# Second graph layer: attributes turned in three pieces, one-hots in PSUM in all rows, last norm in place

## What is computed

```python
gathered = x[edge_col] * edge_vals[:, None]
pre_embed = segment_sum(gathered, edge_row, num_segments=N)
x = layernorm(x + pre_embed @ W.T)              # first layer: not touched by the change
summand = tensor_product(x[src], edge_attr_9, [w0, w1, w2, w3, w4])
x = layernorm(x + segment_sum(summand, dst, N) / sqrt(10))   # second layer
```

## Time and profile before

| what | value |
| --- | --- |
| median of 3 runs | 4139.94 us (4139.83 to 4140.0) |
| the profiled execution's own time | 4139.79 us |
| its span in the profile | 4138.0 us |
| second layer, first to last gather | 1529.47 to 4113.40 us |
| busy over the span: POOL, PE, DVE, ACT | 67%, 58%, 51%, 34% |

### The profile page before, as it was taken

The page is one execution under the profiler, slowest core; times in us unless marked ns, Lnnn a source line. Parts: engine busy times, 40 slices in busy tenths (PEclk is TensorE's granted clock), DMA queues, the critical chain, the costliest instruction groups (busy, mean ns, idle before and its releaser), DMA issues.

```text
span 4138.0 us, 55255 instructions
## 1 busy us (share of the span) xinstructions
PE 2400.2 (58%) x15332; PEld 2126.9 (51%) x15334; DVE 2119.9 (51%) x4357; ACT 1420.4 (34%) x2142; POOL 2769.7 (67%) x2887
## 2 busy tenths in 40 slices
PE   2200199999999964555455554545555455555454
PEld 1000199999999954444444444444444444444443
DVE  8999888888888872232222332322332222323433
ACT  5444366666666651121121211211121111212222
POOL 5100077777777737777777777777777777777775
PEclk6555599999999966677776776767667766776767
DMA  1000133333333332221221222222221221212222
GB/s 58 8 0 20 63 97 96 97 96 98 96 96 92 96 115 59 53 59 53 58 58 53 58 58 53 58 58 53 58 58 53 58 58 52 58 53 73 79 75 57
DMA packets 116447, 268.24 MB, mean 65 GB/s; under 512 B 50449, under 2 KB 50593, under 8 KB 115233
## 3 DMA queue, kind: packets, MB, share of 16 engines
q0 software_dynamic: 92080, 191.02, 17.4%
q1 hardware_dynamic: 19698, 68.09, 4.7%
q10 hardware_dynamic: 4608, 8.39, 0.5%
HBM read 252.30 MB, written 8.72 MB: 63 GB/s over the span
## 4 chain that ended last, share of the span: by engine, by line
POOL 42%; issue 16%; PE 4%; DMA 1%; POOLq 0%; DVE 0%; ACT 0%; DVEq 0%
POOL feat L1565 42%; PE quad L1730 3%; PE mixed L1742 1%; DMA feat<-x,ids 1%; POOLq L1561 0%; POOLq L1562 0%; PE attr_t L1690 0%; ACT z_last L1669 0%; DVE group L1878 0%; DVE dst_col L1965 0%; POOLq L1555 0%; DVE z_last L1976 0%; DVE stats L1979 0%; PE y L1754 0%; POOLq L1559 0%
## 5 line engine op out<-in xcount | busy, mean ns | idle before, releaser
L1565 POOL DMA_INDIRECT feat<-x,ids x2048 | 1960.3, 957 | 636.3 <-issue 632.3
L1730 PE MATMUL quad<-attr_hot,feat 128*128 128x144 f32 x4096 | 919.8, 407 | 1229.4 <-DMA feat<-x,ids 644.3
L1730 PEld LDWEIGHTS quad<-attr_hot,feat 128*128 128x128 f32 x4096 | 860.5, 294 | 1292.9 <-issue 1286.6
L1878 DVE TENSOR_TENSOR group<-group,quad 128x504 f32 (+1 forms) x512 | 347.9, 679 | 1725.5 <-PE quad L1730 1681.5
L1137 POOL DMA_INDIRECT l_feat<-in_x,id_of x768 | 727.7, 948 | 601.7 <-ACT w_of L830 366.4
L1582 ACT ACTIVATE quad<-quad 128x1008 uint32<-128x1008 uint32 x258 | 256.6, 995 | 1834.0 <-DVE group L1878 1834.0
L1742 PE MATMUL mixed<-group,mix 128*128 128x384 f32 x1152 | 414.9, 518 | 17.9 <-DVE group L1878 17.9
L1039 DVE TENSOR_SCALAR keys<-swap,src_of,w_of 128x184 f32<-128x184 f32 x1024 | 327.1, 389 | 93.5 <-PE l_pre L1230 93.5
L1039 DVE TENSOR_SCALAR w_row<-swap,src_of,w_of 128x184 f32<-128x184 f32 x1024 | 327.6, 390 | 51.4 <-PE l_pre L1230 49.7
L1742 PEld LDWEIGHTS mixed<-group,mix 128*128 128x128 f32 x1152 | 235.4, 209 | 171.7 <-issue 49.5
L1211 PE MATMUL got<-x_near,far_w 128*128 128x128 bf16 x4224 | 301.0, 220 | 11.0 <-ACT far_w L847 11.0
(11 more groups left out here) (252 smaller groups left out, 2428.7 us busy)
## 6 DMA issues: line engine op xcount, KB each, us to landing
place<-table SPq DMA_DIRECT2D x64, 640.0 KB
feat<-x,ids POOLq DMA_INDIRECT x2048, 2.5
l_feat<-in_x,id_of POOLq DMA_INDIRECT x768
attr_in<-in_edge_attr SPq DMA_DIRECT2D x18, 576.0 KB, 3.8
norm_x<-in_x SPq DMA_DIRECT2D x16, 256.0 KB, 2.7
x<-norm_z ACTq DMA_DIRECT2D x16, 256.0 KB, 2.4
x_t<-x SPq DMA_DIRECT2D x15, 256.0 KB, 2.7
out<-z_t ACTq DMA_DIRECT2D x15, 256.0 KB, 2.1
```

Source lines behind the costliest of these rows:

```text
L1565: pool.indirect_dma_start(feat[z][:, t, :], None, x1, bass.IndirectOffsetOnAxis(ap=ids[j // (O // 2)][:, c:c + 1], axis=0),).then_inc(feat ...
L1730: last = nc.tensor.matmul(bank[:, :, bass.ds(places[t % H], WIN)], feat[z % S][:, t, :], attr_hot[z % 2][:, t, :, :], start=False, stop=(t ...
L1878: nc.vector.tensor_tensor(to, to, quad[:, q, 0:NA * QUAD_WIN].rearrange("p (m n) -> p m n", m=NA), ALU.add).then_inc(quad_added, 1)
```

## The change

SBUF work space is given up: `off_f` now lies in `attr_hot[0]`, `tile_offs` in `tile_start` itself, `x_last` in `x_t[1]`, and `late_hot`, `z_t` and `z_last` are gone. `attr_t` shrinks from two PSUM banks to one, and the bank won becomes `hots_at`, which holds `hot` and `iota` in all rows, late ones too. The eight attribute matrices are turned four at a time: the first four in row 4 as before, the other four (`turn_rest`) between the halves of row 6, after ScalarE has emptied the bank in row 5; ScalarE copies the second four in row 6. The next attribute load moves with that by two rows. The late batches are summed and normalized in place in `x_t`; their loads wait for the store of the batch two before, and the load of the last batch is issued at the end, after the store of batch 13.

```diff
-off_f = sb("off_f", [P, TN], F32)
-tile_offs = sb("tile_offs", [P, TN // Q, Q - 1], I32)
...
-late_hot = sb("late_hot", [P, R, WIN], F32)
-attr_t = ctx.enter_context(nc.psum_tensor("attr_t", [P, 2, 512], F32))
+attr_t = ctx.enter_context(nc.psum_tensor("attr_t", [P, O // 2 * P], F32))
-loop_hot = y[:, 0:R * WIN].rearrange("p (t n) -> p t n", t=R)
-loop_iota = y[:, R * WIN:R * WIN + WIN]
+hots_at = ctx.enter_context(nc.psum_tensor("hots_at", [P, 512], F32))
+hot = hots_at[:, 0:R * WIN].rearrange("p (t n) -> p t n", t=R)
+iota = hots_at[:, R * WIN:R * WIN + WIN]
+off_f = attr_hot[0][:].rearrange("p t m n -> p (t m n)")[:, 0:TN]
+tile_offs = g.tile_start[:, 0:TN // Q * (Q - 1)].bitcast(I32).rearrange("p (a b) -> p a b", b=Q - 1)
-z_t = [sb(f"z_t{i}", [P, BATCH, D], F32) for i in range(2)]
-x_last = sb("x_last", [P, BATCH, D], F32)
-z_last = sb("z_last", [P, BATCH, D], F32)
+x_last = x_t[1]
...
-    sp.wait_ge(attr_turned, 2)
+    sp.wait_ge(attr_turned, 3)
...
     def load_x(w, e):
-        sp.wait_ge(x_used, w * NE + max(e + 1, 2))
+        sp.wait_ge(stored[e % 2], in_slot(w, e) * 16 + 16)
         sp.dma_start(x_t[e % 2][:], batches(x1)[e]).then_inc(x_here[e % 2], 16)
-    sp.dma_start(x_last[:], batches(x1)[NE]).then_inc(x_last_here, 16)
...
         with sp.Fori(0, LOOPED) as o:
-            sp.wait_ge(attr_turned, w * (2 * OCTETS) + o * 2 + 4)
+            sp.wait_ge(attr_turned, w * (3 * OCTETS) + o * 3 + 6)
             load_attr(o + 2)
...
-            if r % O == TURN_ROW + 1:
-                sp.wait_ge(attr_turned, w * (2 * OCTETS) + (r // O * 2 + 4))
+            if r % O == TURN_ROW + 3:
+                sp.wait_ge(attr_turned, w * (3 * OCTETS) + (r // O * 3 + 6))
                 load_attr((r // O + 2) % OCTETS)
             if r + 1 - EARLY < NE:
                 load_x(w, r + 1 - EARLY)
...
+    sp.wait_ge(stored[1], n_loads * (NE // 2 * 16) + 16)
+    sp.dma_start(x_last[:], batches(x1)[NE]).then_inc(x_last_here, 16)
...
-        nc.scalar.copy(attr_next[:], attr_t[:, 0, 0:O * R]).then_inc(attr_out, 1)
-    def copy_attr(v):
-        for b in range(2):
-            to = attr_e[:, 4 * b:4 * b + 4, :].rearrange("p m t -> p (m t)")
-            nc.scalar.copy(to, attr_t[:, b, :])
-        act.wait_ge(attr_out, v * 2 + 1)
-        nc.scalar.copy(attr_e[:, NA - 1, :], attr_next[:]).then_inc(attr_out, 1)
+        nc.scalar.copy(attr_next[:], attr_t[:, 0:O * R]).then_inc(attr_out, 1)
+    def copy_attr(b):
+        to = attr_e[:, O // 2 * b:O // 2 * (b + 1), :].rearrange("p m t -> p (m t)")
+        nc.scalar.copy(to, attr_t[:]).then_inc(attr_out, 1)
+    def place_last(v):
+        act.wait_ge(attr_out, v * 3 + 1)
+        nc.scalar.copy(attr_e[:, NA - 1, :], attr_next[:])
...
-            done = nc.scalar.activation(z_t[e % 2][:, a, :], z_t[e % 2][:, a, :], ACT.Identity,
+            done = nc.scalar.activation(x_t[e % 2][:, a, :], x_t[e % 2][:, a, :], ACT.Identity,
...
-        act.dma_start(batches(out)[e], z_t[e % 2][:]).then_inc(stored[e % 2], 16)
+        act.dma_start(batches(out)[e], x_t[e % 2][:]).then_inc(stored[e % 2], 16)
...
+    place_last(0)
     copy_attr(0)
+    act.wait_ge(attr_turned, 3)
+    copy_attr(1)
...
             clear_half(0)
+            v = w * OCTETS + o + 1
+            if j == TURN_ROW + 2:
+                act.wait_ge(attr_turned, v * 3 + 3)
+                copy_attr(1)
             if e is not None:
                 normalize(w, e)
...
             if j == TURN_ROW + 1:
-                act.wait_ge(attr_turned, w * (2 * OCTETS) + o * 2 + 4)
+                act.wait_ge(attr_turned, v * 3 + 2)
                 act.wait_ge(hot_made, u + (O - 1 - j) + 2)
-                copy_attr(w * OCTETS + o + 1)
+                place_last(v)
+                copy_attr(0)
...
         if j == TURN_ROW:
-            pe.wait_ge(attr_out, v * 2 + 1)
+            pe.wait_ge(attr_out, v * 3 + 1)
             pe.sem_inc(g.turn, 1)
-            turn_attr(range(NA - 1))
+            turn_attr(range(0, O // 2))
+    def turn_rest(v, j):
+        if j == TURN_ROW + 2:
+            pe.wait_ge(attr_out, v * 3 + 2)
+            pe.sem_inc(g.turn, 1)
+            turn_attr(range(O // 2, NA - 1))
...
-        if e == 0:
-            pe.wait_ge(hot_made, u + 3)
...
-            for h in range(2):
-                half_row(w, r, h, j, n_fill)
+            half_row(w, r, 0, j, n_fill)
+            turn_rest(w * OCTETS + o + 1, j)
+            half_row(w, r, 1, j, n_fill)
             if j % 2 == 0 and not (first and j == 0):
...
             half_row(w, r, 0, r, r // S)
             if batch_of(r) is not None:
                 turn_nodes(w, w * RN + r, batch_of(r))
+            turn_rest(w * OCTETS + (r // O + 1), r % O)
             half_row(w, r, 1, r, r // S)
...
-        link(nc.vector.tensor_tensor(off4[:, :, 1:Q], by4[:, :, 1:Q],
-                                     by4[:, :, 0:1].to_broadcast([P, TN // Q, Q - 1]), ALU.subtract))
         nc.vector.memset(row_offs[:], 0)
-        link(nc.vector.tensor_scalar(tile_offs[:], off4[:, :, 1:Q], keep, None, ALU.mult))
         link(nc.vector.tensor_tensor(offq, quad_first, quad_first[:, :, 0:1].to_broadcast([P, RN, R // Q]),
                                      ALU.subtract))
         link(nc.vector.tensor_scalar(row_offs[:, 0:RN, 1:Q], offq[:, :, 1:Q], keep, None, ALU.mult))
-        link(nc.vector.tensor_scalar(off_f[:], starts, keep, None, ALU.mult))
-        nc.vector.tensor_tensor(g.dst_rel[:], g.dst_col[:], off_f[:], ALU.subtract)
-        link(nc.vector.tensor_copy(g.row_f[:], off_f[:].rearrange("p (a b) -> p a b", b=R)[:, :, 0]))
+        link(nc.vector.tensor_scalar(off_f, starts, keep, None, ALU.mult))
+        link(nc.vector.tensor_tensor(g.dst_rel[:], g.dst_col[:], off_f, ALU.subtract))
+        link(nc.vector.tensor_copy(g.row_f[:], off_f.rearrange("p (a b) -> p a b", b=R)[:, :, 0]))
         link(nc.vector.tensor_copy(row_offs[:, START_LAG:RN + START_LAG, 0], g.row_f[:]))
+        link(nc.vector.tensor_tensor(off4[:, :, 1:Q], by4[:, :, 1:Q],
+                                     by4[:, :, 0:1].to_broadcast([P, TN // Q, Q - 1]), ALU.subtract))
+        link(nc.vector.tensor_scalar(tile_offs, off4[:, :, 1:Q], keep, None, ALU.mult))
...
-    def hots(u, r, j, z, late=False):
-        hot = late_hot[:] if late else loop_hot
-        iota = g.cst[:, C_IOTA:C_IOTA + WIN] if late else loop_iota
+    nc.vector.tensor_copy(iota, g.cst[:, C_IOTA:C_IOTA + WIN]).then_inc(iota_made, 1)
+    dve.wait_ge(iota_made, 1)
+    def hots(u, r, j, z):
...
         dve.wait_ge(x_here[e % 2], in_slot(w, e) * 16 + 16)
-        dve.wait_ge(stored[e % 2], in_slot(w, e) * 16 + 16)
-        nc.vector.tensor_tensor(z_t[e % 2][:], x_t[e % 2][:], y[:].rearrange("p (a d) -> p a d", a=BATCH),
+        nc.vector.tensor_tensor(x_t[e % 2][:], x_t[e % 2][:], y[:].rearrange("p (a d) -> p a d", a=BATCH),
                                 ALU.add).then_inc(x_used, 1)
...
-                dve.wait_ge(attr_out, w * (2 * OCTETS) + o * 2 + 4)
+                dve.wait_ge(attr_out, w * (3 * OCTETS) + o * 3 + 6)
             r = o * O + (j + 2)
-            hots(w * RN + r, r, (j + 2) % O, j % 2, late)
...
-        nc.vector.tensor_copy(loop_iota, g.cst[:, C_IOTA:C_IOTA + WIN]).then_inc(iota_made, 1)
-        dve.wait_ge(iota_made, w + 1)
-        dve.wait_ge(attr_out, w * (2 * OCTETS) + 2)
+        dve.wait_ge(attr_out, w * (3 * OCTETS) + 3)
...
-                next_hots(r // O, r % O, late=True)
+                next_hots(r // O, r % O)
```

More of the change, by code:

```diff
@@ L1647, in row @@
                     if j == TURN_ROW - 1:
-                        act.wait_ge(attr_turned, w * (2 * OCTETS) + o * 2 + 3)
+                        act.wait_ge(attr_turned, v * 3 + 1)
                         copy_last()
                     if j == TURN_ROW + 1:
-                        act.wait_ge(attr_turned, w * (2 * OCTETS) + o * 2 + 4)
+                        act.wait_ge(attr_turned, v * 3 + 2)
                         act.wait_ge(hot_made, u + (O - 1 - j) + 2)
-                        copy_attr(w * OCTETS + o + 1)
+                        place_last(v)
+                        copy_attr(0)
                 for j in range(O):
@@ L1668, in _ @@
             for a in range(BATCH):
-                done = nc.scalar.activation(z_last[:, a, :], z_last[:, a, :], ACT.Identity, bias=shift[:, a:a + 1],
+                done = nc.scalar.activation(x_last[:, a, :], x_last[:, a, :], ACT.Identity, bias=shift[:, a:a + 1],
                                             scale=rstd[:, a:a + 1])
@@ L1672, in _ @@
             act.wait_ge(last_normed, 1)
-            act.dma_start(batches(out)[NE], z_last[:]).then_inc(last_stored, 16)
+            act.dma_start(batches(out)[NE], x_last[:]).then_inc(last_stored, 16)
             passes_run = act.value_load(g.n_pass[0:1, 1:2], min_val=1, max_val=g.PASSES1)
@@ L1689, in turn_attr @@
                 for n, m in enumerate(ms):
```

(25 more changed lines are left out.)

## The result

The changed kernel takes 4116.74 us, median of 5 runs (4115.77 to 4118.43), against 4139.94 (4137.57 to 4140.87); the ratio of the two is 0.9945 with a 95% interval of 0.9931 to 0.996. The profiled execution took 4116.74 us, its span 4115.0, which is 23.0 us less than before.

The account below looks back on a forecast made before the run. POOL was taken to bound the kernel at 1.249 us a gather. From 4139.8 us, -23.5 (one-hots) and +0.1 (tables), the rest 0, gave 4116.4; the median stands 0.15 higher, so 4116.5 us, range 4114.5 to 4120.

Parts of the forecast that it names:

- The signs that were named for being right: Late gathers average 944 ns, none after the tables over 1 us, last gather ends near 4090, four first gathers still stretched.
- One-hots, -23.5 us: Late rows: with `iota` and `hot` in PSUM, 235 gathers fall from 1.349 to 1.249 us each, saving 23.5 us.
- Tables, +0.1 us (bounds -0.5 and +0.7): Start of the stage: reordered table steps stretch the first gathers by 4.0 or 2.8 us in place of 3.3.
- my two cases: Start of the stage: the first gather waits for the 512 subtraction or slips in just ahead, 4.0 or 2.8 us.
- Three-piece turning, 0 us: Row 6 of each octet: ScalarE's first copy is done 4.4 us early, so TensorE doesn't wait between the halves.
- the second cover: Row 6 of octets: if TensorE did wait, the gathers' half slots would hide a lag of some 20 us from POOL.
- In place, 0 us: Late batches: `x_t` reloads with 30 us to spare; `x_last` loads two rows (40 us) before the last gather ends.

Follow-up runs that it names:

- late_both: Changed kernel with both late-row one-hot steps reading and writing SBUF again (count in constants, hot in its own SBUF buffer): 4138.79 us.
- all_sbuf: Changed kernel with the one-hots in SBUF in all 128 rows, looped ones too: 4327.86 us, single run.
- late_product: Changed kernel with the late rows' hot in SBUF but the count still in PSUM, so only the product has two SBUF operands: 4137.92 us.
- psum_tables: Changed kernel with start tables rebuilt: steps have at most one SBUF tensor input and write or read PSUM; ScalarE clears `quad` after the tables: 4113.07 us.
- old_tables: Changed kernel with the start tables' order and buffers of before, the 1536 subtraction and scaling at the head: 4115.35 us.
- lag8: Changed kernel with ScalarE's first copy of four delayed by 8 chained copies in row 5 of each octet: 4115.78 us, single run.
- lag19: Changed kernel with ScalarE's first copy of four delayed by 19 chained copies in row 5 of each octet: 4190.76 us, single run.
- changed_again: The changed kernel itself, unaltered, run once more on the same chip as the rebuilt-tables kernel: 4115.94 us.

## Why the prediction was right

- **The bound.** POOL's pitch, 1.249 us a gather, held in every kernel wherever no gather was held; what changed the time is what lengthened or held a gather. The forecast was 4116.5 us, the median 4116.74. The signs that were named for being right came: 943 ns in the late rows, no long gather after the tables, the last gather's end at 4089.6.
- **One-hots, -23.5 us.** Measured -23.6 in the late rows. late_both and all_sbuf show that it is these steps, late_product that it is the 2.56 us product, psum_tables that the same kind of step costs nothing with one operand in PSUM. That the place of the operands was the only difference between looped and late rows was argued in the prediction; it is shown now.
- **Tables, +0.1 us (bounds -0.5 and +0.7).** Measured +0.9, outside the bounds and small. The first gather did not slip in ahead of the 512 subtraction: it started 0.16 us before it and was held all the same (1.88 us). That is the dearer of my two cases, 4.0 us; I had taken the middle. What goes beyond it lies in the fourth gather, which I let go on at the end of the 1536 subtraction: it ended 1.17 us after that, not 0.82, with the scaling from 1537.00 right behind, and 0.12 us after that scaling. That the scaling held it a second time fits, but was not tried by itself. old_tables shows that the order makes the 0.9.
- **Three-piece turning, 0 us.** In row 6 of the octets TensorE never waits for the copy, with 4.0 us to spare where I had read 4.4; its one wait for it, 0.9 us, lies at the start of the stage. lag8 and lag19 bear out the second cover: 11 us of waiting are hidden, 32 are not. I had put too little there: a wait of some 28 us is hidden in an octet, where I had some 20. The copy could come 32 us late (36 of lag19 less the 4 that each octet lost), not 25.
- **In place, 0 us.** The loads of the batches now wait on SP, and no wait of VectorE for `x_t` shows. The load of the last batch is issued at 4070.59, 18 us before the last gather starts and 37 before its sum at 4107.75; I had put it two rows (40 us) ahead of the last gather's end, and overlooked that on SP it stands behind the attribute load, which waits for the turning in row 126 and is issued at 4069.39. Hidden all the same.
- **What cancelled.** Against +0.9 at the start stand -0.2 ahead of the stage and -0.9 in the pitch; the +0.8 behind the last gather goes with the execution and not with the kernel (below). The total is closer to the forecast than its parts; that much is luck.
- **The rule weighed.** By the Trainium skill, "SBUF — State Buffer", section "Who interferes with whom", a `tensor_tensor` would not hold up descriptor generation, by an inference marked there as one. The runs go against the inference: late_product has one such step in each of 14 rows and gives back 21.6 us. The same section also says that a VectorE instruction with two SBUF inputs contends with a GpSimd instruction that reads SBUF, and each gather here reads its ids from SBUF; with that sentence the trace agrees.

## What to carry to other kernels

Where POOL issues indirect DMAs one after the other and nothing waits in between, look for gathers that last longer than their neighbours and see which VectorE step ends 0.8 us before they do. Give a step with two inputs one of them in PSUM: its own time may stay the same, and the gather beside it gets its usual length. A scaling from SBUF to SBUF can write to PSUM instead; in psum_tables that made the step itself longer (2.27 us). A wait put into a deeply buffered consumer is free up to the buffers' depth, and beyond it costs only the rest; but in the last round no later gathers hide it (11.5 us in lag19).

## What was not expected of the hardware

- The hold is not even. The late products of the earlier trace rows took at most 2571 ns beside gathers, 14 more than their shortest, so VectorE hardly waits for POOL; a gather that begins inside such a product waits to its end. A gather that has begun before the product mostly goes on, as late_product showed. The one exception is the first gather of the stage, which began 0.16 us before the 512 subtraction and was held to its end; what sets it apart is open.
- Behind the last gather the last mix took 7.74 us in the changed kernel and 6.04 before, with the same 18 products. The granted clock says why; TensorE in the stretch of the mix (start and end; length, busy us (count), clock, DMA share, GB/s), before and after, with four single microseconds of after:

```profile
4121.00:4128.00 7.00, 6.04 (x18) 1.00 0.00 1
```

```profile
4096.00:4105.00 9.00, 7.74 (x18) 0.81 0.00 0
...
4094.00:4095.00 1.00, 0.81 (x6) 0.98 0.00 0
...
4098.00:4099.00 1.00, 1.00 (x3) 0.50 0.00 0
4099.00:4100.00 1.00, 1.00 (x3) 0.50 0.00 0
...
4101.00:4102.00 1.00, 1.00 (x4) 1.00 0.00 0
```

Before, the whole mix ran at 1.00, the level of 2.4 GHz. After, the clock had risen earlier, near 4094 and still in the half row ahead of the mix, which took 3.58 us in place of 4.18. TensorE then stood for 2 us, as before, and after about 0.7 us of the mix the clock fell to 0.50, the level of 1.2 GHz, for some 3 us. The change did not do this: changed_again is the same kernel, and there the mix ran at 1.00 throughout and the stretch behind the last gather took 25.3 us, as before (25.5).

```profile
4097.00:4104.00 7.00, 6.04 (x18) 1.00 0.00 0
```

In old_tables, all_sbuf and psum_tables the clock falls within the mix again, which takes 7.74 us there too. Why it falls in one execution and not in another is open and was not tried.
